# Expert tiles in reverse slot order, and two scatter-adds in flight, in a conv + attention + mixture-of-experts layer

## What is computed

```
x = x + conv_gate(group_norm(x))              # 8 images, 512 channels, 16x16
t = tokens(x)                                 # 8 x 256 tokens of 512
t = t + attention(layer_norm(t))              # 16 heads of 32, soft cap, window 256
xf = layer_norm(t)                            # 2048 tokens
scores = softmax(xf @ gate_w.T)               # 8 experts
w, i = top_k(scores, 2);  w = w / sum(w)
y = sum over the two chosen experts e of  w_e * ((silu(xf @ wg[e]) * (xf @ wu[e])) @ wd[e])
shared = (silu(xf @ sg) * (xf @ su)) @ sd
out = t + y + shared
```

## Time and profile before

| | us |
|---|---|
| median of 3 runs (lowest, highest) | 765.47 (764.77, 766.08) |
| time of the profiled execution | 765.3 |
| its span, from the first to the last instruction | 763.5 |
| around the span | 1.8 |
| PE busy in the span | 646.3 (85%) |
| POOL busy | 277.9 (36%) |
| the 39 scatter-adds: from the start of the first to the start of the last | 557.47 to 751.96 |

### The profile page before, as it was taken

The page is one execution under the profiler, slowest core; times in us unless marked ns, Lnnn a source line. Parts: engine busy times, 40 slices in busy tenths (PEclk is TensorE's granted clock), DMA queues, the critical chain, the costliest instruction groups (busy, mean ns, idle before and its releaser), DMA issues.

```text
span 763.5 us, 13600 instructions
## 1 busy us (share of the span) xinstructions
PE 646.3 (85%) x4859; PEld 523.7 (69%) x4860; DVE 423.2 (55%) x1022; ACT 262.0 (34%) x462; POOL 277.9 (36%) x324
## 2 busy tenths in 40 slices
PE   0001269999999999999999999999799999999991
PEld 0000168888888888888779899999566766776670
DVE  7898634665657574846555897223444444444440
ACT  7340005554536363545543222534222112212210
POOL 1780002333223232323231113765345445544531
PEclk9999999999999999999999999999899999999997
DMA  9450000000101010102025533351755565556543
GB/s 304 139 164 0 0 1 1 2 29 29 55 0 55 0 55 0 55 0 85 2 83 198 175 111 112 111 166 42 275 87 97 105 109 96 99 108 100 99 65 40
DMA packets 24786, 62.08 MB, mean 81 GB/s; under 512 B 3056, under 2 KB 7152, under 8 KB 23728
## 3 DMA queue, kind: packets, MB, share of 16 engines
q1 hardware_dynamic: 15344, 41.16, 15.7%
q0 software_dynamic: 8736, 20.45, 15.2%
q10 hardware_dynamic: 672, 0.03, 0.1%
HBM read 38.56 MB, written 23.07 MB: 81 GB/s over the span
## 4 chain that ended last, share of the span: by engine, by line
PE 55%; DMA 25%; DVE 12%; issue 4%; ACT 1%; POOL 1%; SPq 0%; DVEq 0%; POOLq 0%
PE PS L1396 24%; DMA out_tokens<-yo,dest 24%; PE scores L1396 12%; PE scores L1629 5%; PE PS L1491 4%; PE scores L1476 4%; PE PS L1446 2%; DVE v L888 2%; DVE col L899 1%; PE PS L1435 1%; DMA T<-in_x 1%; ACT probs L650 1%; DVE col L903 1%; DVE qT L828 1%; DVE col L904 1%
## 5 line engine op out<-in xcount | busy, mean ns | idle before, releaser
L1396 PE MATMUL scores<-xb,sw 128*128 128x256 f32 x768 | 97.7, 283 | 0.0
L1396 PEld LDWEIGHTS scores<-xb,sw 128*128 128x128 f32 x768 | 95.1, 191 | 2.3 <-issue 0.6
L575 POOL DMA_INDIRECT out_tokens<-yo,dest x39 | 61.8, 1584 | 92.8 <-DMA out_tokens<-yo,dest 90.6
L491 POOL TENSOR_SCALAR_AFFINE_SELECT probs<-probs 128x256 f32<-128x256 f32 x128 | 50.1, 426 | 117.6 <-ACT probs L657 117.5
L1396 PE MATMUL PS<-xt_h,w_h 128*128 128x256 f32 x256 | 75.5, 295 | 1.5 <-DVE xt_l L1047 1.5
L1710 PE MATMUL scores<-wd_sb,ehT 128*128 x156 | 73.5, 593 | 1.0 <-DVE ehT L1356 1.0
L1396 PE MATMUL PS<-xt_l,w_h 128*128 128x256 f32 x256 | 73.3, 286 | 0.0
L1396 PE MATMUL PS<-xt_h,w_l 128*128 128x256 f32 x256 | 73.2, 286 | 0.0
L779 ACT ACTIVATE es<-scores 128x256 f32<-128x256 f32 x39 | 15.0, 384 | 164.2 <-PE scores L1396 164.2
L1396 PE MATMUL scores<-wgu_h,xgT_h 128*128 x156 | 65.7, 421 | 4.4 <-DVE xgT_l L1360 4.4
L1352 DVE TENSOR_TENSOR eh<-scores,es 128x256 f32<-128x256 f32 x39 | 16.6, 425 | 87.7 <-ACT es L779 87.7
(11 more groups left out here) (255 smaller groups left out, 1351.2 us busy)
## 6 DMA issues: line engine op xcount, KB each, us to landing
wgu_l<-in_wgu SPq DMA_DIRECT2D x8, 1024.0 KB, 6.9
T<-in_x SPq DMA_DIRECT2D x8, 512.0 KB, 8.2
probs<-in_wqkvo SPq DMA_DIRECT2D x8, 512.0 KB, 3.7
x_rows<-x SPq DMA_DIRECT2D x8, 512.0 KB, 2.8
x_cols<-x2T SPq DMA_DIRECT2D x8, 512.0 KB, 2.7
xc<-x_cols SPq DMA_DIRECT2D x8, 512.0 KB, 3.7
out_tokens<-T SPq DMA_DIRECT2D x8, 512.0 KB, 7.4
wd_sb<-in_wd SPq DMA_DIRECT2D x8, 512.0 KB, 6.8
```

The lines of the kernel that those rows point to most:

```text
L491: ins = pool.affine_select(out=t, in_=t, compare_op=ALU.is_ge, fill=0.0, base=0, pattern=[[0, 2], [1, P]], channel_multiplier=-1)
L575: pool.indirect_dma_start(out[:, :], bass.IndirectOffsetOnAxis(dest[:, t:t + 1], 0), yo[:, t % 3, :], None, compute_op=ALU.add).then_inc(y ...
L1396: ins = pe.matmul(out, lhs(k, a), rhs(k, b), start=m == 0, stop=m == len(products) - 1)
```

## The change

- Tiles are worked off in reverse slot order: `pair_slots` replaces a slot's tile by 38 minus the tile, `tile_experts` works out the expert of each turn accordingly. The four unused tiles come first (turns 0 to 3), then experts 7 down to 0; expert 0 has the turns 35 to 38.
- `tile_experts` also computes for each turn a number `landed_for`: 16 if the turn before is a tile of the same expert (then nothing need have landed), otherwise the count that the semaphore of turn t-1's buffer has when scatter-add t-1 has landed. With the counts above it asks for that landing in the turns 1 to 4, 8, 12, 16, 21, 25, 30 and 35.
- `scatter_add(t)` waits for that number, which POOL loads into a register after each scatter-add. Two tiles of one expert hold different tokens and may be in flight together.
- `yo` has two buffers and each its own landing semaphore; `expert_out(t)` waits for scatter-add t-2.
- The spare rows are written by POOL in two transfers of 64 rows instead of by SP in one of 128.
- DVE's expert loop is unrolled by two turns rather than three. PE's stream is the same.

```diff
+                dve.wait_ge(dve_step, step_of(dve.tensor_scalar(slot_f[:, 1, :], slot_f[:, 1, :], -1.0,
+                                                                float(NTILES - 1), ALU.mult, ALU.add)))
...
             def tile_experts():
-                dve.wait_ge(dve_step, step_of(dve.tensor_tensor(
-                    te[:, :, :], iota_f[0:1, 0:NTILES].unsqueeze(2).to_broadcast([1, NTILES, E]),
-                    s8[0:1, 2, :].unsqueeze(1).to_broadcast([1, NTILES, E]), ALU.is_ge)))
-                dve.wait_ge(dve_step, step_of(dve.tensor_reduce(te_f[:, :], te[:, :, :], AX.X, ALU.add)))
-                dve.tensor_scalar(tile_expert[:, :], te_f[:, :], -1.0, None, ALU.add).then_inc(experts_ready, 1)
+                step_of(dve.tensor_tensor(ends[:, 1, :], s8[0:1, 2, :], s8[0:1, 1, :], ALU.add))
...
+                dve.tensor_scalar(landed_for[:, :], strict[:, 1, :], 16.0, None, ALU.add).then_inc(firsts_ready, 1)
...
-                if b == 3:
-                    sp.wait_ge(dn_free, 1)
-                    sp.dma_start(out[B * S:B * S + P, :], at(T, 0)[:, 0:C]).then_inc(residual_stored[0], 16)
...
-            def scatter_add(t):
+            def landing_count(t):
+                return pool.value_load(landed_for[0:1, t:t + 1], min_val=16, max_val=16 + 16 * (NTILES // YO + 1))
+
+            def scatter_add(t, landed):
                 if t == 0:
                     for b in range(B):
-                        pool.wait_ge(residual_stored[b], 16 if b else 32)
+                        pool.wait_ge(residual_stored[b], 16)
+                    for k in range(YO):
+                        pool.wait_ge(y_landed[k], 16)
                 else:
-                    pool.wait_ge(y_added, 16 * t)
+                    pool.wait_ge(y_landed[(t - 1) % YO], landed)
+                    stand_alone(pool)
                 pool.wait_ge(yo_ready, t + 1)
-                pool.indirect_dma_start(out[:, :], bass.IndirectOffsetOnAxis(dest[:, t:t + 1], 0), yo[:, t % 3, :],
-                                        None, compute_op=ALU.add).then_inc(y_added, 16)
+                pool.indirect_dma_start(out[:, :], bass.IndirectOffsetOnAxis(dest[:, t:t + 1], 0), yo[:, t % YO, :],
+                                        None, compute_op=ALU.add).then_inc(y_landed[t % YO], 16)
+                return landing_count(t + 1) if t + 1 < NTILES else None
+
+            pool.wait_ge(dn_free, 1)
+            for k in range(YO):
+                pool.dma_start(out[B * S + 64 * k:B * S + 64 * (k + 1), :],
+                               at(T, 0)[64 * k:64 * (k + 1), 0:C]).then_inc(y_landed[k], 16)
...
                 if not (isinstance(uses, int) and uses == 0):
-                    dve.wait_ge(y_added, 16 * (t - 2))
+                    dve.wait_ge(y_landed[k], 16 + 16 * uses)
...
-            pool.wait_ge(y_added, 16 * NTILES)
+            for k in range(YO):
+                pool.wait_ge(y_landed[k], 16 + 16 * len(range(k, NTILES, YO)))
```

More of the change, by code:

```diff
@@ L33 @@
 RANGE = 128.0
-NPAIR = NH // 2
+YO = 2
 HC = P // D
@@ L128, in layer_kernel @@
         tile_expert = sb("tile_expert", [1, NTILES], u32)
+        landed_for = sb("landed_for", [1, NTILES], i32)
         PROBS, SMALL, BATCH = 4 * 2 * 384, 1840, CB * S
@@ L234, in layer_kernel @@
         te_f = sb("te_f", [1, NTILES], fp32, scope)
+        te_is = sb("te_is", [1, NTILES, E], fp32, scope)
+        ends = sb("ends", [1, 2, E], fp32, scope)
+        strict = sb("strict", [1, 4, NTILES], fp32, scope)
+        strict_i = sb("strict_i", [1, 2, NTILES], i32, scope)
         ex = sb("ex", [P, 4, NT], fp32, scope)
@@ L264, in layer_kernel @@
         ehT = sb("ehT", [P, I], fp32, scope)
-        yo = sb("yo", [P, 3, C], fp32, scope)
+        yo = sb("yo", [P, YO, C], fp32, scope)
         scope.close()
@@ L318, in layer_kernel @@
             sem("chosen_ready"), sem("prefix_full"), sem("gap_exp"))
-        onehot_ready, onehot_used, ids_ready, experts_ready = (
-            sem("onehot_ready"), sem("onehot_used"), sem("ids_ready"), sem("experts_ready"))
+        onehot_ready, onehot_used, ids_ready, experts_ready, firsts_ready = (
+            sem("onehot_ready"), sem("onehot_used"), sem("ids_ready"), sem("experts_ready"), sem("firsts_ready"))
         xg_loaded = [sem(f"xg_loaded{k}") for k in range(3)]
@@ L325, in layer_kernel @@
             sem("hT_full"), sem("hT_ready"), sem("ey_full"), sem("yo_ready"))
-        y_added = sem("y_added")
+        y_landed = [sem(f"y_landed{k}") for k in range(YO)]
         residual_stored = [sem(f"residual_stored{b}") for b in range(B)]
@@ L580, in _ @@
             pool.wait_ge(ids_ready, 2)
+            pool.wait_ge(firsts_ready, 1)
             low_with_weights(6, (), (0, 1, 2))
@@ L583, in _ @@
             weight_low(13)
+            landed = None
             for t in range(3, NTILES):
@@ L586, in _ @@
                 if t >= 5:
-                    scatter_add(t - 5)
+                    landed = scatter_add(t - 5, landed)
             for t in range(NTILES - 5, NTILES):
-                scatter_add(t)
-            pool.wait_ge(y_added, 16 * NTILES)
+                landed = scatter_add(t, landed)
+            for k in range(YO):
+                pool.wait_ge(y_landed[k], 16 + 16 * len(range(k, NTILES, YO)))
         @block.scalar
@@ L750, in _ @@
                     if b == 5 and j == 0:
-                        act.wait_ge(residual_stored[0], 32)
+                        for k in range(YO):
+                            act.wait_ge(y_landed[k], 16)
+                        act.wait_ge(residual_stored[0], 16)
                         act.wait_ge(residual_stored[1], 16)
@@ L1270, in tile_experts @@
-                dve.wait_ge(dve_step, step_of(dve.tensor_reduce(te_f[:, :], te[:, :, :], AX.X, ALU.add)))
-                dve.tensor_scalar(tile_expert[:, :], te_f[:, :], -1.0, None, ALU.add).then_inc(experts_ready, 1)
+                step_of(dve.tensor_tensor(ends[:, 1, :], s8[0:1, 2, :], s8[0:1, 1, :], ALU.add))
+                dve.wait_ge(dve_step, n.value())
+                dve.wait_ge(dve_step, step_of(dve.tensor_scalar(ends[:, 0, :], ends[:, 1, :], -1.0, float(NTILES),
+                                                                ALU.mult, ALU.add)))
@@ new lines, in tile_experts @@
+                turn = iota_f[0:1, 0:NTILES]
+                for t, op in ((te, ALU.is_ge), (te_is, ALU.is_equal)):
+                    step_of(dve.tensor_tensor(t[:, :, :], turn.unsqueeze(2).to_broadcast([1, NTILES, E]),
+                                              ends[:, 0, :].unsqueeze(1).to_broadcast([1, NTILES, E]), op))
+                dve.wait_ge(dve_step, n.value())
+                step_of(dve.tensor_reduce(te_f[:, :], te[:, :, :], AX.X, ALU.add))
+                step_of(dve.tensor_reduce(strict[:, 0, :], te_is[:, :, :], AX.X, ALU.max))
@@ new lines, in tile_experts @@
+                dve.wait_ge(dve_step, n.value())
+                dve.wait_ge(dve_step, step_of(dve.tensor_scalar(strict[:, 1, :], te_f[:, :], -1.0, float(E), ALU.mult,
+                                                                ALU.add)))
+                dve.tensor_scalar(tile_expert[:, :], strict[:, 1, :], float(E - 1), None,
+                                  ALU.min).then_inc(experts_ready, 1)
+                step_of(dve.tensor_scalar(strict[:, 2, :], te_f[:, :], 0.0, None, ALU.is_equal))
@@ new lines, in tile_experts @@
+                dve.wait_ge(dve_step, n.value())
+                step_of(dve.tensor_tensor(strict[:, 3, :], strict[:, 0, :], strict[:, 2, :], ALU.max))
+                step_of(dve.tensor_scalar(strict_i[:, 0, :], turn, 8.0, 8.0, ALU.mult, ALU.add))
+                dve.wait_ge(dve_step, n.value())
+                dve.wait_ge(dve_step, step_of(dve.tensor_scalar(strict_i[:, 1, :], strict_i[:, 0, :], 4, 4,
+                                                                ALU.logical_shift_right, ALU.logical_shift_left)))
@@ L1273, in one_hots @@
+                dve.wait_ge(dve_step, step_of(dve.tensor_copy(strict[:, 0, :], strict_i[:, 1, :])))
+                dve.wait_ge(dve_step, step_of(dve.tensor_tensor(strict[:, 1, :], strict[:, 0, :], strict[:, 3, :],
+                                                                ALU.mult)))
+                dve.tensor_scalar(landed_for[:, :], strict[:, 1, :], 16.0, None, ALU.add).then_inc(firsts_ready, 1)
             def one_hots(g):
@@ L1365, in expert_out, with tile_steps @@
                 if not (isinstance(uses, int) and uses == 0):
-                    dve.wait_ge(y_added, 16 * (t - 2))
+                    dve.wait_ge(y_landed[k], 16 + 16 * uses)
                 dve.tensor_scalar(yo[:, k, :], ey_bank, slot_w[:, bass.ds(t, 1)], None, ALU.mult).then_inc(yo_ready, 1)
[L1369 to L1378, removed]
+            def tile_steps(t, odd, pair, start=False, end=False):
+                hidden(t)
+                if not end:
+                    x_low(t + 1)
+                if not start:
```

(10 more changed lines are left out.)

## The result

The changed kernel takes 760.33 us (median of 4 runs, 760.19 to 760.72), the kernel before 765.12 us beside it on the same chip (764.32 to 766.08): ratio 0.9938, interval 0.9920 to 0.9955. The gain is 4.8 us where 1.9 were forecast, and the time lies 2.5 us under the range. The profiled execution took 760.72 us with a span of 758.9, against 765.3 and 763.5 before.

The account below looks back on a forecast made before the run. The prediction took PE to bound the expert stretch, with landings just in time. Its terms, 765.3 - 2.33 + 0.2 + 0.21, gave 763.4 us, 763.6 on the median's scale, with a range of 762.8 to 765.4.

Parts of the forecast that it names:

- What bounds the kernel: Expert stretch: PE leads at 5.13 us a turn, landings come just in time, so the change wins nothing in its body.
- The last scatter-add: End of the expert stretch: turn 38's scatter-add waits for `yo` alone and leaves 0.29 us behind it, 2.33 us earlier.
- Rival 1: End of the expert stretch: the last scatter-add leaves 0.81 us behind `yo`, as now; 764.1 us, chance 0.2.
- Then the end is fixed ... I take these as unchanged: After POOL's last wait at 756.7 us: its closing drain of 6.44 us stays as it was.
- the last landing: End of the expert stretch: a used tile now lands last, charged 0.2 us, bounds -0.1 and +0.3.
- Spare rows, "0": Before `hl` of image 4: POOL's two added issues fit into an idle gap of 3.45 us; cost 0.
- tile_experts, 0 with a thin cover: DVE before `hf` of image 4: twelve more instructions, 3.0 us, leave PE 0.37 us to spare; cost 0, bounds 0 and +1.0.
- pair_slots, +0.21: Chain to the first one-hots, where PE already stands still: one more 128x32 instruction costs 0.21 us.
- Register loads, 0: POOL's turns: 38 loads of 0.30 us each are hidden in 1.97 us free a turn; cost 0.
- Rival 3: Expert stretch: register loads make POOL the bound, each of 38 turns 0.53 us longer at 2.5 us; 784 us, chance 0.08.
- Rival 2: End of the expert stretch: the last scatter-add still leaves at some 752.0 us, added costs remain; 765.9 us, chance 0.08.

Follow-up runs that it names:

- e2_const_sp: The changed kernel with its eleven landing waits written as constants, no register loads, and the spare rows on SP as before; 762.12 us.
- g2: e2_const_sp with three semaphore increments added on POOL behind the last scatter-add; 763.53 us.
- h1: e2_const_pool with the two spare-row DMAs counted on semaphores of their own instead of the landings' semaphores; 763.87 us.
- h2: The kernel before with the spare rows on POOL in two DMAs, counted on the scatter-adds' own semaphore; 762.47 us.
- e3: The kernel before with only the spare rows moved from SP to POOL, in two DMAs on two semaphores of their own; 764.81 us.
- e1: The changed kernel with every turn waiting for the landing of the turn before, so that scatter-adds are serial again; 783.97 us.
- e2_const_pool: The changed kernel with its eleven landing waits written as constants and no register loads, the spare rows still on POOL; 760.42 us.
- g3: The changed kernel with ten semaphore increments added on POOL behind the last scatter-add; 760.92 us.
- i1: The changed kernel with five spare-row DMAs instead of two, so that the gathers' three semaphores also count a plain DMA each; 760.96 us.
- i2: The kernel before with the spare rows on POOL in three DMAs, counted on the gathers' three semaphores alone; 762.55 us.
- i3: e2_const_pool with both spare-row DMAs counted on the first of the two landing semaphores; 760.60 us, from two runs.

## Why the prediction was wrong

**What bounds the kernel: right.** PE leads the expert stretch, the landings were spare time, and the change wins nothing there. PE's 40.00 of 40 us and its turn of 5.13 are unchanged.

**The last scatter-add: right, 2.16 us where 2.33 were forecast.** The choice of 0.29 against 0.81 behind `yo` was right: 0.28 where the turn waits for no landing, and more (0.64 to 0.90) at the later turns where it does (8, 12, 16, 21, 25, 30, 35). The rule of the Trainium skill (Perfetto Trace Analysis, "DMA Instruction — SWDGE (GPSIMD)") that gave 2.33 is borne out by these 0.28. The very last one left 0.46 behind `yo`, nearer to 0.29 than to 0.81; that is the missing 0.17. Rival 1, at 0.81, is out.

**"Then the end is fixed ... I take these as unchanged": the step that failed.** POOL's DRAIN fell from 6.44 to 3.75 us, 2.69 us that the sum did not have. It was put at no change without a reason, although the change touches POOL's DMAs and their semaphores. With the long DRAIN the rest of the sum comes out: the three kernels that keep it and have the change's order and its eleven waits took 762.12, 763.53 and 763.87 us (e2_const_sp, g2, h1), about the 763.6 forecast. The other part of that stretch was mis-sized a little: from the last scatter-add to the branch it is 5.2 us instead of 4.74, so +0.5 instead of the +0.2 charged for the last landing. Over all kernels the 0.2 holds: this stretch is 4.80 to 5.21 with the reversed order (eleven kernels, middle one 4.84) and 4.47 to 4.81 with the old one (eight, middle 4.68). The profiled execution of the change has the longest of them all. The range was also drawn a little off its own words: 763.3 less half of 1.3 is 762.65 and not 762.8, which changes nothing here.

**Spare rows, "0": the edit that did it.** The step counted the issues and found them hidden, which they are: both DMAs lie in POOL's idle gap, and the `hl` behind them came at 474.48, still ahead of PE's first down product at 475.75. What it did not ask is what else the edit changed: the two plain DMAs now count on the semaphores of the scatter-adds. That is worth all of the 2.69: between h2 and e3, with the same two DMAs, it is 2.82 us, and the two DMAs by themselves lengthen the DRAIN by 0.13 (e3 against the kernel before).

```profile
469.04 1.01 DVE L1299 TENSOR_TENSOR te_is<-iota_f,ends 1x312 f32<-1x312 f32 x1
...
469.66 1.36 POOL L594 DMA_DIRECT2D out_tokens<-T  x2
...
473.53 0.42 DVE L1136 TENSOR_TENSOR hf<-scores,sg 128x256 f32<-128x256 f32 x1
...
474.48 0.74 POOL L504 TENSOR_TENSOR hl<-hf,hh 128x256 fp32r<-128x256 f32 x1 [3.46 <-ACT hh L745]
475.75 0.63 PE L1681 MATMUL scores<-sw,hh 128*128 128x512 f32 x2
```

**tile_experts, 0 with a thin cover: right.** `hf` of image 4 starts at 473.53, forecast 473.63, and PE's product at 475.75, where the kernel before has 475.73. One of its instructions was stretched (`te_is`, 1.01 us instead of 0.47), and the cover held.

**pair_slots, +0.21: right.** PE's stall ahead of the first `place` grew from 0.82 to 1.02:

```profile
434.67 0.55 PE L1711 MATMUL PS<-oh_tile,oh_row 128*128 128x120 f32 x3 [1.02 <-DVE oh_tile L1337]
```

Yet the last `yo` ended 0.21 earlier than before, not later, so the sign of that line of the table comes from elsewhere. From one profile each this can't be told from the spread: the last `yo` ended between 747.92 and 750.13 in the variants other than e1.

**Register loads, 0: right.** Line 572, one load for each turn but the first (ns min/median/max):

```profile
L572 POOLq TENSOR_LOAD <-landed_for x38: 282/289/498, 557.0 to 745.9; - x38
L572 POOLq FUSED_REGOPS  x38: 147/147/188, 557.6 to 746.2; - x38
L572 POOLq SEQ_ASSERT  x38: 18/18/32, 557.8 to 746.4; - x38
```

That is 0.29 us where PE's row gave 0.30, and half of the floor that the Trainium skill (DMA: Bandwidth & Descriptors, "Latency and other measured facts") states. Rival 3 is out for this change. In e1, where every turn waits, POOL's chain does become the bound, but by the landing and the 0.8 us behind it and not by loads; that its time is rival 3's 784 is chance. Rival 2 is out: POOL left for the last scatter-add 2.16 us earlier behind its data.

## What to carry to other kernels

The time behind the last DMA is a stage of its own: read the closing DRAIN of each engine in the profile and don't book it as a constant, least of all when the change moves DMAs to that engine or changes what they count on. When an edit "only" moves an issue, ask which semaphore it increments as well as when it runs. And where two chains run at one pace, removing waits from the slower-looking one wins only at the end of the stretch, while half a microsecond added to each of its steps can cost nearly twenty (e1).

## What the runs showed of the hardware

- POOL's closing DRAIN took 3.75 to 3.87 us in the eight kernels where a plain and an indirect DMA of POOL count on a common semaphore (after, e1, e2_const_pool, g3, h2, i1, i2, i3), and 6.44 to 6.56 us in the eleven where none does. The number of instructions (512 to 733 recorded), of register loads (0 to 38) and of DMAs, the overlap and the order of the scatter-adds made no such difference. Why a shared semaphore shortens it is open: nothing in the traces shows what POOL does in that time; no engine is busy and no DMA packet moves in it (DMA share 0.00 from 756.8 to 763.2 us before, from 754.9 to 758.6 after). Whether the plain DMA has to come first, as it did in all eight, was not tried. In all eight ACT and POOL also wait on the shared semaphore for the spare rows, which in the eleven they do on another; no run sets these waits apart from the count.
- Plain DMAs add to the DRAIN: two on their own semaphores 0.126 us (6.563 in e3 against 6.437 before), three more on shared ones 0.122 (3.868 in i1 against 3.746 in the change).
- In the kernels in which only eleven turns wait for a landing the last scatter-add left 0.46 to 0.47 us behind `yo` where the spare rows go through POOL, and 0.28 where they go through SP (e2_const_sp, g2). No run explains the 0.18.
- A wait that is an instruction of its own ahead of an indirect DMA costs some 0.8 us from the releaser to the issue (0.81 behind `yo` before, 0.82 behind the landings of e1), one that the DMA carries 0.27 to 0.31 in the rows shown and 0.46 at the change's last turn. Over e1's chain of 39 this step makes 5.6 us of a landing's 4.8, and the time 784 us where the kernel before takes 765.
